# Group statistics taken where a layer's output is made, in a four-layer network on one core

## The reference, cut to what matters

```
for layer in (gru, attention, experts, attention):
    g = x grouped: 16 images, 196 tokens, 32 groups of 6 channels
    n = (x - mean(g)) / sqrt(var(g) + 1e-5)      # per image and group
    x = x + layer(n)
```

## Time and profile before

| | us |
|---|---|
| median of 3 runs | 1919.51 (1915.17 to 1924.06) |
| profiled execution | 1919.37 |
| its span, from the first to the last instruction | 1917.6 |
| PE busy | 1503.1 (78%) |
| DVE busy | 1313.1 (68%) |
| ACT busy | 951.3 (50%) |
| POOL busy | 740.5 (39%) |
| mean granted clock of TensorE | 0.788 of 2.4 GHz |

### The profile page before, as it was taken

How to read it: one execution, slowest core, us unless ns; L and a number is a source line. 1 busy time by engine, 2 the same in 40 slices (tenths; PEclk the granted TensorE clock), 3 DMA queues, 4 the chain that set the end, 5 groups by cost and what they waited for, 6 DMA issues and landing times. The chain is left out here.

```text
span 1917.6 us, 51586 instructions
## 1 busy us (share of the span) xinstructions
PE 1503.1 (78%) x19477; PEld 1286.0 (67%) x19477; DVE 1313.1 (68%) x4844; ACT 951.3 (50%) x1918; POOL 740.5 (39%) x675
## 2 busy tenths in 40 slices
PE   4778888888845878889756899599994288888887
PEld 4667777777734867767544677388883277676766
DVE  7788888888857478778646674344444655787874
ACT  3633333333335577778614234344442256787881
POOL 3700000000022167779733012345550405686994
PEclk9955555555576999999885579799996589999998
DMA  2000000000032686668142204312224358676832
GB/s 82 4 4 4 4 4 4 4 4 4 4 106 87 164 232 147 147 126 148 26 127 74 90 25 162 117 57 66 63 63 147 103 156 225 140 165 127 161 59 58
DMA packets 62671, 167.20 MB, mean 87 GB/s; under 512 B 16648, under 2 KB 40184, under 8 KB 59740
## 3 DMA queue, kind: packets, MB, share of 16 engines
q1 hardware_dynamic: 57052, 151.05, 31.6%
q0 software_dynamic: 5376, 12.85, 2.3%
HBM read 95.84 MB, written 67.42 MB: 85 GB/s over the span
## 5 line engine op out<-in xcount | busy, mean ns | idle before, releaser
L903 POOL TENSOR_TENSOR l_arena<-l_arena,l_arena 98x784 fp32r<-98x784 f32 x192 | 354.7, 1860 | 110.0 <-PE l_ps L1012 72.5
L434 PE MATMUL gru_ps_r<-gru_hp,gru_wp 128*128 128x16 f16 x3920 | 200.5, 176 | 70.3 <-DVE gru_hp L406 69.5
L434 PEld LDWEIGHTS gru_ps_r<-gru_hp,gru_wp 128*128 128x128 f16 x3920 | 150.8, 105 | 92.0 <-DVE gru_hp L406 89.9
L842 POOL MEMSET l_arena<- 32x6272 f32 x2 | 10.6, 5319 | 511.3 <-POOLq L45 511.3
L1180 DVE TENSOR_REDUCE l_ps<-l_ps 98x4 f32<-98x784 f32 x192 | 187.5, 976 | 25.1 <-PE l_ps L973 20.2
L434 PE MATMUL gru_ps_n<-gru_hp,gru_wp 128*128 128x16 f16 x3920 | 191.2, 174 | 0.0
L1011 PE MATMUL l_ps<-l_arena,l_arena 128*66 128x196 f32 x768 | 163.1, 265 | 24.5 <-POOL l_arena L903 24.2
L489 ACT ACTIVATE gru_tr<-gru_ps_r,gru_unscale 128x32 f32<-128x32 f32 x196 | 56.4, 288 | 220.5 <-PE gru_ps_r L434 220.5
L1123 ACT ACTIVATE l_arena<-l_ps 98x784 fp32r<-98x784 f32 x192 | 158.4, 825 | 4.6
L1126 ACT ACTIVATE l_arena<-l_ps 98x784 f32<-98x784 f32 x192 | 157.0, 818 | 0.0
L1012 PE MATMUL l_ps<-l_arena,l_arena 128*66 128x196 f32 x768 | 156.3, 257 | 0.0
(11 more groups left out here) (344 smaller groups left out, 4642.7 us busy)
## 6 DMA issues: line engine op xcount, KB each, us to landing
l_arena<-qk SPq DMA_DIRECT2D x48, 588.0 KB
qk<-l_arena SPq DMA_DIRECT2D x48, 392.0 KB, 7.3
rel<-l_arena SPq DMA_DIRECT2D x24, 686.0 KB
l_arena<-rel SPq DMA_DIRECT2D x24, 686.0 KB
l_arena<-x SPq DMA_DIRECT2D x32, 294.0 KB, 6.4
qk<-l_arena SPq DMA_DIRECT2D x12, 784.0 KB, 14.4
l_arena<-in_experts_dram SPq DMA_DIRECT2D x8, 1152.0 KB, 7.5
l_arena<-picked SPq DMA_DIRECT2D x16, 294.0 KB
```

The lines of the kernel that those rows point to most:

```text
L434: last = pe.matmul(out[:, b, B * m:B * m + B], wp[:, wi, g, m, :], hp[:, b, part, B * k:B * k + B], start=False, stop=True, skip_group_che ...
L903: pool.tensor_tensor(pl[:TH, g % 2, :, :], p32[:TH, g % 2, :, :], ph[:TH, g % 4, :, :].bitcast(f32), ALU.subtract).then_inc(pl_ready, 1)
```

## The change

Layers 1 and 2 take `bn_stats` and `bn_aggr` of their own output tiles as they are made (`Moments.tile`), into an SBUF tensor `moments` [128, 2, 16, 2] that outlives the layers. Layers 2 and 3 don't take statistics; they use `moments` with averaging matrices for the layout of the layer that made them (to find `dev`) and for their own (to find mean and variance). Their square root is preceded by one on a single column. In layer 3 the weights are loaded ahead of x; in layer 2 the shared expert's weights are rounded and subtracted between images. Layer 0 and layer 1's own head are as they were.

```diff
+    def spread_of_groups(self, dve, mean_sums, source_sums):
+        dve.memset(self.eps[:, :], EPS).then_inc(self.eps_ready, 1)
+        dve.wait_ge(self.source_ready, 1)
+        dve.tensor_copy(self.mean_s[:, :, :].rearrange("p k b -> p (k b)"), source_sums).then_inc(self.mean_copied, 1)
...
+        dve.wait_ge(self.mean_ready, 1)
+        dve.tensor_copy(self.mean_g[:, :, :].rearrange("p k b -> p (k b)"), mean_sums).then_inc(self.mean_copied, 1)
+    def tensor_given(self, pe, mean_sums, var_sums, source_sums):
+        pe.wait_ge(self.avg_in, 32)
+        for m in range(2):
+            for k in range(2):
+                last = pe.matmul(source_sums[:, m * B:(m + 1) * B], self.avg[:, k, m, :], self.moments[:, k, :, 0], start=k == 0, stop=k == 1)
...
+class Moments:
+    def tile(self, dve, x, n, added):
+        dve.wait_ge(added, 2 * n + 2)
+        for b in (2 * n, 2 * n + 1):
+            for k, width in enumerate(self.widths):
+                dve.bn_stats(self.stats[:width, k, b, :], x(k, slice(b * T, (b + 1) * T))).then_inc(self.chan, 1)
+        dve.wait_ge(self.chan, 4 * n + 4)
+        for b in (2 * n, 2 * n + 1):
+            for k, width in enumerate(self.widths):
+                dve.bn_aggr(self.moments[:width, k, b, :], self.stats[:width, k, b, :]).then_inc(self.ready, 1)
@@ attention_layer, SyncE, given (layer 3) @@
+                    sp.dma_start(norm.avg, ins["avg128"]).then_inc(norm.avg_in, 16)
+                    sp.dma_start(norm.avg_out, ins["avg_back"]).then_inc(norm.avg_in, 16)
+                    load_weights()
+                    norm.load_x(sp, x_in)
@@ attention_layer, DVE, kept (layer 1), after the additions of tile n @@
+                    if kept is not None and n >= 1:
+                        new_moments.tile(dve, lambda k, cols: xy[:CP, k, cols], n - 1, added)
+                if kept is not None:
+                    new_moments.tile(dve, lambda k, cols: xy[:CP, k, cols], NT - 1, added)
@@ route, POOL, after image b @@
+                    if b in (10, 12, 14):
+                        pool.wait_ge(lb_ready, b + 1)
+                        weight_low(b // 2 - 5)
@@ route, ACT @@
+                act.activation(warm[:, :], eps[:, :], ACT.Sqrt).then_inc(warm_ready, 1)
                 act.wait_ge(var_ready, 1)
                 act.activation(std[:, :, :].rearrange("p k b -> p (k b)"), var_sums, ACT.Sqrt, bias=eps[:, :]).then_inc(std_ready, 1)
-                act.wait_ge(ahead_in, 32)
-                act.activation(wh[:, :, :, :], w13[:, :, :, :], ACT.Copy).then_inc(high_ready, 1)
-                act.activation(w2h[:, :, :], w2s[:, :, :], ACT.Copy).then_inc(high_ready, 1)
                 act.wait_ge(shift_ready, 1)
                 for b in range(B + 2):
+                    if b == 9:
+                        act.wait_ge(ahead_in, 32)
+                        act.activation(wh[:, :, :, :], w13[:, :, :, :], ACT.Copy).then_inc(high_ready, 1)
+                    if b == 11:
+                        act.activation(w2h[:, :, :], w2s[:, :, :], ACT.Copy).then_inc(high_ready, 1)
@@ mixture, DVE, after the additions of tile n - 1; and at the end @@
+                    if n >= 2:
+                        new_moments.tile(dve, lambda k, cols: xs[:CHUNKS[k][1], k, cols], n - 2, added)
...
+                for n in (NT - 2, NT - 1):
+                    new_moments.tile(dve, lambda k, cols: xs[:CHUNKS[k][1], k, cols], n, added)
```

More of the change, by code:

```diff
@@ L70, in __init__ @@
             del shapes["xn"]
+        if moments is not None:
+            del shapes["stats"], shapes["mv"]
+            shapes.update(dev=[128, 2, B], spread=[128, 2, B], mean_s=[128, 2, B], avg=[128, 2, 2, 128], avg_out=[128, 2, CB, CP], eps=[CP, 1])
         if place is None:
@@ L136, in normalize @@
             if b < B:
+                if self.moments is not None and b % self.CHUNK == 0:
+                    dve.wait_ge(self.x_chunk[b // self.CHUNK], 16 * CB)
                 if b >= 2:
@@ L159, in gpsimd @@
             self.low(pool, b, 1)
+    def tensor_given(self, pe, mean_sums, var_sums, source_sums):
[3 more added lines that the diff above has]
+                last = pe.matmul(source_sums[:, m * B:(m + 1) * B], self.avg[:, k, m, :], self.moments[:, k, :, 0], start=k == 0, stop=k == 1)
+        last.then_inc(self.source_ready, 1)
+        for m in range(CB):
+            for k in range(2):
+                last = pe.matmul(mean_sums[:, m * B:(m + 1) * B], self.avg_out[:, k, m, :], self.moments[:, k, :, 0], start=k == 0, stop=k == 1)
+        last.then_inc(self.mean_ready, 1)
+        pe.wait_ge(self.spread_ready, 1)
+        for m in range(CB):
+            for k in range(2):
+                last = pe.matmul(var_sums[:, m * B:(m + 1) * B], self.avg_out[:, k, m, :], self.spread[:, k, :], start=k == 0, stop=k == 1)
+        last.then_inc(self.var_ready, 1)
     def tensor(self, pe, mean_sums, var_sums):
@@ L169, in scalar @@
         act.wait_ge(self.eps_ready, 1)
+        if self.moments is not None:
+            act.activation(self.std[:, 0, 0:1], self.eps[:, :], ACT.Sqrt).then_inc(self.std_ready, 1)
+            act.wait_ge(self.std_ready, 1)
         act.wait_ge(self.var_ready, 1)
@@ L173, in scalar @@
         for b in range(B):
+            if self.moments is not None and b % self.CHUNK == 0:
+                act.wait_ge(self.x_chunk[b // self.CHUNK], 16 * CB)
             for k in range(CB):
@@ L1232, in route @@
     with Scope(nc, "ro") as s:
[L1233 to L1235 removed]
+        mean, std, rstd, shift = (s.sb(n, [128, 2, B]) for n in "mean std rstd shift".split())
+        mean_s, dev, spread = (s.sb(n, [CP, CB, B]) for n in "mean_s dev spread".split())
+        avg, avg_out, eps, warm = s.sb("avg", [CP, CP]), s.sb("avg_out", [CP, CB, 2, 128]), s.sb("eps", [128, 1]), s.sb("warm", [128, 1])
         g = s.sb("g", [128, 2, E])
@@ L1293, in _ @@
                                        ALU.subtract).then_inc(lb_ready, 1)
+                    if b in (10, 12, 14):
+                        pool.wait_ge(lb_ready, b + 1)
+                        weight_low(b // 2 - 5)
             @block.tensor
             def _(pe):
-                pe.wait_ge(const_in, 48)
-                pe.wait_ge(chan2, 2 * B)
+                pe.wait_ge(avg_in, 32)
+                pe.matmul(source_sums, avg[:, :], moments[:CP, :, :, 0], start=True, stop=True).then_inc(source_ready, 1)
                 for m in range(2):
-                    for k in range(2):
-                        last = pe.matmul(mean_sums[:, m * B:(m + 1) * B], avg[:, k, m, :], mv[:, k, :, 0], start=k == 0, stop=k == 1)
+                    for k in range(CB):
+                        last = pe.matmul(mean_sums[:, m * B:(m + 1) * B], avg_out[:, k, m, :], moments[:CP, k, :, 0], start=k == 0, stop=k == 1)
                 last.then_inc(mean_ready, 1)
@@ L1304, in _ @@
                 for m in range(2):
-                    for k in range(2):
-                        last = pe.matmul(var_sums[:, m * B:(m + 1) * B], avg[:, k, m, :], spread[:, k, :], start=k == 0, stop=k == 1)
+                    for k in range(CB):
+                        last = pe.matmul(var_sums[:, m * B:(m + 1) * B], avg_out[:, k, m, :], spread[:, k, :], start=k == 0, stop=k == 1)
                 last.then_inc(var_ready, 1)
```

148 lines of the change are left out of this document (95 added, 53 removed).

## The result

The changed kernel takes 1894.16 us, the median of 4 runs (1889.1 to 1898.72), where the kernel before took 1918.88 beside it: ratio 0.986, 95% interval 0.983 to 0.989. Two more sets of runs of the same kernel gave 0.985 (0.982 to 0.988) and 0.9845 (0.982 to 0.987); over all 14 runs its mean is 1891.0. The forecast was 1888, range 1877 to 1902. The sign and the two places are as forecast, and the size is within the range; not all terms of the sum came out, and one thing that nobody forecast, an earlier rise of the clock in the middle of layer 2, brought the sum nearer.

The account below looks back on a forecast made before the run. Between barriers, the heads of layers 2 and 3 leave TensorE idle; in layer 2's routing loop TensorE sets the pace. Sum: 1919.37 - 26.6 + 1.5 + 1.4 + 1.6 - 9 = 1888.3 us, range 1877 to 1902.

Parts of the forecast that it names:

- Layer 1's tail (+1.4): End of layer 1: DVE's added moments delay its last division and TensorE, 1.4 us longer; ends 0 and 4.
- Layer 2's head (-26.6): Start of layer 2: without statistics and work ahead of the first image, TensorE starts at T+10.5 against T+37.1, 26.6 us less.
- The weights inside the loop (+1.5): Layer 2's routing loop: weight work between images, ACT and POOL catch up, blocked DVE costs 1.5 us.
- its groups keep 1.05 us but for a gap near images 11 to 15: Layer 2's routing loop, sign of being right: TensorE's groups hold their pace except near the inserted weight work.
- Layer 2's tail (+1.6): End of layer 2: moments of tile 5 stand ahead of the last two additions, 1.55 us; ends 1 and 4.
- Layer 3's head (-9): Start of layer 3: normalization starts at 16.4 against 27.2, less 1.5 for POOL's later splits: 9 us less.
- the two named: Layer 3's head: DVE's first weight cast and subtraction, forecast to be stretched to about 3 us by POOL's two casts.
- what I took of POOL's later splits, 1.5: Layer 3's head: POOL's splits of the last weights fall into the normalization, counted as costing only 1.5 us.
- layer 3's head gives nothing: Rival: in layer 3, late x, blocked DVE and POOL's later splits take the gain; 1897 us, chance 0.12.
- slower: the clock: Rival: TensorE stays at 1.2 GHz longer after a head; with 80 us more cold work 1928 us, chance 0.02.

Follow-up runs that it names:

- the run with the weights first: Changed kernel with layer 2's shared expert weights rounded and subtracted ahead of the first image again, as before the change: 1909.09 us, ratio 0.994 to the kernel before.
- the layer-3 half: Kernel before with only layer 3's new head and the keeping of moments in layer 2: 1917.28 us over 10 runs, ratio 0.9997.
- the halves and repairs: Layer 2's or layer 3's new head alone (ratios 0.989, 0.9997); eight row buffers, k casts on ScalarE, last moments later, together on the changed kernel (0.9815, 0.983).

## Why the prediction was right, and where its terms were not

**Layer 1's tail (+1.4):** +0.7 from the division ahead of the first moments (960.31; 961.20 before) to the next stage (31.65 in place of 30.93). Right in kind, half in size: the first tile of moments pushed the next division by 1.3, but the 0.3 per tile after it didn't come (they follow every 4.1 as before), and 0.75 was regained behind the last division.

**Layer 2's head (-26.6):** the chain up to the first image was right to 0.8 us: source mean at T+4.2 (3.4 forecast), normalization at T+9.2 (8.7), TensorE at T+11.3 (10.5), so -25.8. The 0.8 goes with the second matrix, which landed 3.8 after its issue where 2.5 was taken.

**The weights inside the loop (+1.5):** the loop grew by 3.7. Some 1 of it is the weights' work, within my term. The other 2.7 is the step that failed: I counted each queue's landing of x and weights, but not what stands behind them on it. Before, the first store came over 37 us into the stage; the change brings it to T+12.9 (1004.87), 2.4 behind the issue of the last weights. By their shapes x (256 x 3136) and the weights (128 x 2816) are 4.7 MB, and they land only at T+19.9, as the run with the weights first showed. The run with eight buffers gives this back (3.2). My list of things "late next" held engines and no store. So the sign "its groups keep 1.05 us but for a gap near images 11 to 15" failed: the largest gap, 2.7, came ahead of the fifth image.

**Layer 2's tail (+1.6):** +1.55 (36.98 in place of 35.43 to the next stage, from VectorE's mixing step behind its last long wait for ScalarE, at 1426.32 and 1454.44).

**Layer 3's head (-9):** the start was right to 0.4 us (16.0), with some luck. Two instructions were blocked, as forecast, but not the two named: the first cast began 0.13 ahead of POOL's and ran at its own length (0.56), and the second one, of 128x384, was held in its place (2.95). Mis-sized was what I took of POOL's later splits, 1.5: between the start, 11 won, and the attention loop, 5.6 won, some 5 are lost, and the held operations of the first images are the rows that grew. No run took just these splits away, so their share is read from rows and not shown by itself; TensorE's wait for a DMA just ahead of the loop also grew, from 3.2 and 4.1 to 4.6 as a mean. The reason I gave, that DVE was idle there, was read from a head in which TensorE was the late one; with DVE ahead of it the lock falls on the critical chain. Eight profiles with this head have the attention loop start at + 104.9 as a mean (103.2 to 106.8), two without it at + 110.5: -5.6. And layer 3 as a whole takes 424.7 in place of 427.9 as means: -3.2. The loop itself ran 2.4 longer with the early start. TensorE's waits for its DMAs (`l_arena<-l_arena`) from the loop's first step on sum to 4.2 and 3.9 us in the two without the new head and to 4.9 to 6.3 (5.6 as a mean) in the eight with it, so some 1.6 of the 2.4 are such waits; why they grow, and the rest, is open. The rival "layer 3's head gives nothing", to which I gave 0.12, is nearer to this than my term: with the tail's 1.6 the layer-3 half wins 1.6, and by its own run 0.4 with an interval from -3.8 to +2.7.

**Unforecast, in its favour: the mixture,** 3.7 shorter as a mean of three profiles of the changed kernel against one before, though it now holds the 1.6 of the kept moments: 5.3 by the earlier rise of the clock, which may be chance (the table above). The rival "slower: the clock" named the mechanism with the sign turned.

**The sum.** Local terms as measured: +0.7 - 22.2 + 1.6 - 3.2 = -23.1; the measured difference of the means is 1891.0 - 1919.7 = -28.7 (43 runs of the kernel before). The rest, 5.6, is of the size of what the clock does between executions. The forecast of -31 was thus met by terms that were 8 too large in sum and a gain of 5.6 it didn't know. That the sum came so near is luck; the sign, both places and the chain up to the first image are not.

## What to carry to other kernels

When a head is shortened, what stood safely behind it now meets its loads: look through each DMA queue for the first store and count the bytes ahead of it against the buffers that wait for it. POOL's casts and subtractions cost VectorE's casts, `tensor_scalar` and two-input operations up to their full length wherever VectorE is the late one, and a gap in VectorE's timeline before the change is no cover after it; put such work on ScalarE, or where VectorE waits for something else. Statistics that VectorE takes on a tile just made cost 1.5 us each and vanish beside a loop bound by others; only the last ones show.

The length of one head resolves 1 us (51.6 to 52.4 in three profiles), where all of layer 3 spread over 4 and the total by more: the halves and repairs here were told apart by heads, hardly one of them by its total. And two delays that lie side by side hide each other: taking away the statistics alone won 7 of the 22 here, and the rest came only with the weights' work out of the way.

## What the runs showed of the hardware

With identical instructions the mixture took 418.9 or 421.6, and over kernels that differ there by 1.6 us of work at most it took 418.8 to 426.0, by when the granted clock rose for good, 47 to 69 us after its start. That is more than any single edit here moved, but for the head of layer 2. In the run with TensorE kept busy the clock fell within a gap of 5 us in TensorE's work, and the 50 us of nearly unbroken matmuls behind the gap didn't raise it. The Trainium skill (TensorE: Matmul & The Clock Gate, "The HAM clock gate") says that how many matmuls run at the lower clock at a kernel's start varies from run to run of one kernel. The rise inside this kernel varies too, by far more: 47, 57 and 64 us in the three profiles of the changed kernel. It also says that the clock follows how busy TensorE has been; the stretch from 994.03 to 1044, with TensorE busy for 46 of 50 us and the clock at 0.50 throughout, does not agree, and why is open.

POOL's lock on VectorE holds across neighbouring POOL instructions: 7.06 for 1.25 us of work. It held under a POOL memset too, which reads nothing, for `tensor_scalar` (1.97 in place of 0.67 at 1489.90, ending with the memset at 1491.46). Two-input operations beside a memset were not held: 32-element ones kept their 0.19 to 0.20 beside that of 1468.67 to 1471.38, and, in the run with the k casts on ScalarE, two subtractions of 96x196 their 0.62.

```profile
1468.67 2.71 POOL L924 MEMSET l_arena<- 1x3136 f32 x1
...
1470.03 0.20 DVE L122 TENSOR_TENSOR l_arena<-to_moments,l_arena 128x32 f32<-128x32 f32 x1
```

```profile
1491.18 0.62 DVE L182 TENSOR_TENSOR l_arena<-l_arena,l_arena 96x196 fp32r<-96x196 f32 x2
...
1491.20 1.86 POOL L937 MEMSET l_arena<- 128x2112 f32 x1
```
